# A graph network on one core: epsilon inside the square roots, a first phase begun by the features and not the lists, six chains there, and padding that isn't gathered

## The reference

```python
x = layernorm(x + attention(x, src, dst))         # Q, K, V = x W + b, 8 heads of 16
#   score = exp(clip(sum(K[src] * Q[dst]) / 4, -5, 5)); segment_sum(V[src] * score) / (segment_sum(score) + 1e-6)
x = layernorm(x + gin(x, src, dst, edge_attr_64)) # messages (x[src] + mlp(edge_attr)) / sqrt(deg deg), node mlp,
#   out * rsqrt(mean(out * out) + 1.19e-7) * rms_w
x = layernorm(x + equivariant(x, edge_attr_3, edge_weight, src, dst))
x = layernorm(x + gat(x, src, dst))               # exp(leaky(f_src[src] + f_dst[dst]) - segment_max), f_v[src]
layernorm(x) = (x - mean(x)) / sqrt(var(x) + 1e-5)
```

## Time and profile before

| | us |
|---|---|
| median of 3 runs (lowest, highest) | 4626.52 (4621.08, 4627.65) |
| the profiled execution | 4619.58 |
| its span, first to last instruction | 4614.9 |
| first gather to last gather, pass 1, 2, 3, 4 | 59.1 to 1098.5, 1181.3 to 2235.9, 2356.8 to 3396.9, 3469.7 to 4509.6 |
| first load of x (ACT's queue), issue | 0.71 |
| loads of x1, x2, x3 (SP's queue), issue | from 0.72, 4.83 in all |
| second and last load of the lists (SP's queue), issue | 12.93 |

### The profile page before, as it was taken

How to read it: one execution, slowest core, us unless ns; L and a number is a source line. 1 busy time by engine, 2 the same in 40 slices (tenths; PEclk the granted TensorE clock), 3 DMA queues, 4 the chain that set the end, 5 groups by cost and what they waited for, 6 DMA issues and landing times.

```text
span 4614.9 us, 103452 instructions
## 1 busy us (share of the span) xinstructions
PE 3700.7 (80%) x25659; PEld 3147.4 (68%) x25659; DVE 3313.9 (72%) x7588; ACT 2856.1 (62%) x7389; POOL 3271.2 (71%) x3435
## 2 busy tenths in 40 slices
PE   6888888887376666666769888888888999999996
PEld 4555555555376666666658677677677888888886
DVE  4666666667554444444668777777787999999998
ACT  3777676766532222222357666666656888888886
POOL 4777777775677777777657777777747777777772
PEclk8898898888587777777879999999999999999998
DMA  7888888884443333333122222222228887888882
GB/s 231 246 234 239 236 233 239 236 236 146 112 100 76 82 81 77 82 77 81 42 62 57 57 56 56 56 56 57 56 76 243 236 235 234 235 235 234 234 235 77
DMA packets 645495, 677.23 MB, mean 147 GB/s; under 512 B 126761, under 2 KB 511295, under 8 KB 645247
## 3 DMA queue, kind: packets, MB, share of 16 engines
q0 software_dynamic: 133120, 327.79, 27.2%
q1 hardware_dynamic: 509838, 346.88, 25.1%
q10 hardware_dynamic: 2416, 1.18, 0.1%
HBM read 584.73 MB, written 89.08 MB: 146 GB/s over the span
## 4 chain that ended last, share of the span: by engine, by line
POOL 27%; issue 21%; PE 16%; DVE 12%; ACT 11%; DMA 7%; SPq 2%; ACTq 2%; DVEq 1%; POOLq 0%
POOL e_rows L852 19%; POOL xt L852 8%; PE banks L914 7%; DVE acc L938 5%; ACT e_away L891 4%; DMA xt<-up_t,e_index 3%; PE banks L1032 3%; DVE banks L1482 2%; ACT e_logit L1478 1%; ACT banks L1544 1%; DMA e_q_rows<-q_t 1%; DMA e_rows<-kv_t,e_index 1%; ACTq L944 1%; ACT e_rows L1543 1%; PE banks L437 1%
## 5 line engine op out<-in xcount | busy, mean ns | idle before, releaser
L938 DVE TENSOR_TENSOR acc<-acc,banks 128x256 f32 x3328 | 1383.3, 416 | 886.1 <-PE banks L914 749.3
L852 POOL DMA_INDIRECT xt<-up_t,e_index x800 | 757.3, 947 | 243.7 <-issue 213.0
L852 POOL DMA_INDIRECT e_rows<-x_t,e_index x772 | 730.3, 946 | 248.0 <-issue 232.8
L852 POOL DMA_INDIRECT e_rows<-fsv_t,e_index x772 | 730.1, 946 | 236.0 <-issue 217.9
L852 POOL DMA_INDIRECT e_rows<-kv_t,e_index x772 | 730.1, 946 | 235.3 <-issue 220.7
L1174 ACT ACTIVATE e_rows<-banks,e_rows 128x128 f32<-128x128 f32 x832 | 236.9, 370 | 726.5 <-DMA e_rows<-x_t,e_index 481.0
L914 PE MATMUL banks<-e_sel,e_msg 128*128 128x128 f32 (+1 forms) x3328 | 654.5, 312 | 0.0
L1165 PE MATMUL banks<-e_w,xt 65*128 65x128 f32 x1664 | 273.2, 317 | 350.8 <-DMA xt<-in_attr_rows 346.7
L914 PEld LDWEIGHTS banks<-e_sel,e_msg 128*128 128x128 f32 (+1 forms) x3328 | 356.3, 148 | 262.6 <-issue 171.3
L891 ACT ACTIVATE e_away<-node_iota,local 128x128 f32<-128x128 f32 x1664 | 526.0, 388 | 0.0
L1165 PEld LDWEIGHTS banks<-e_w,xt 65*128 65x128 f32 x1664 | 248.6, 229 | 359.5 <-issue 308.0
(11 more groups left out here) (193 smaller groups left out, 7046.3 us busy)
## 6 DMA issues: line engine op xcount, KB each, us to landing
e_q_rows<-q_t SPq DMA_DIRECT2D x832, 64.0 KB
sel_d<-e_sel_t SPq DMA_DIRECT2D x208, 256.0 KB
e_sel_t<-sel_d SPq DMA_DIRECT2D x208, 256.0 KB
e_far<-fdst_t SPq DMA_DIRECT2D x832, 64.0 KB
e_near<-near_d SPq DMA_DIRECT2D x208, 128.0 KB
xt<-in_attr_rows SPq DMA_DIRECT2D x208, 128.0 KB, 3.6
e_resets<-reset_d SPq DMA_DIRECT2D x208, 128.0 KB
xt<-up_t,e_index POOLq DMA_INDIRECT x800
```

The lines of the kernel that those rows point to most:

```text
L852: G.indirect_dma_start(out=self.rows[:, u, i, 0:self.width], out_offset=None, in_=self.table, in_offset=bass.IndirectOffsetOnAxis(ap=index ...
L938: V.tensor_tensor(to, to, bank[n_bank][:, col:col + W].rearrange("p (k d) -> p k d", k=2), ALU.add).then_inc(self.s_added[i], 1)
```

## The change

Four edits. **Roots:** the scale is now ACT's immediate scale and the epsilon its bias column, made once by POOL (`ln_eps`, `rms_eps`); the instruction on DVE and its step in the plan are gone. **First phase:** the weights go first on ACT's queue, in three groups with a semaphore each (keys and values, their biases, the queries' own); all loads of x go on SP's queue, and the two loads of the integer rows (the lists) stand behind the first two of them. The planner gives the lists a start of 8.0 and the key/value chains 0.0, and there are six chains and not three. **Padding:** in the last group the chunk without edges isn't gathered, and of the chunk with 10 edges only 10 rows are. The wait for a group's rows counts the gathers that there are.

```diff
     def tables(...):
-        for lo, sem in zip(range(0, FULL_TILES, X_TILES), loaded_x):
-            (SP if lo else A).dma_start(x[:, lo:lo + X_TILES, :], ...).then_inc(sem, 16)
+        load_w(0, "k", loaded_kv)
+        load_w(1, "v", loaded_kv)
+        load_b(0, "k", loaded_b)
+        load_b(1, "v", loaded_b)
+        load_w(2, "q", loaded_q)
+        load_b(2, "q", loaded_q)
         G.memset(x[:, FULL_TILES:, :], 0.0).then_inc(cleared_x, 1)
-        SP.wait_ge(cleared_x, 1)
-        SP.dma_start(x[0:REST, FULL_TILES, :], ...).then_inc(loaded_x[-1], 16)
-        for n, name in enumerate(("k", "v", "q")):
-            A.dma_start(w_qkv[:, n * D:(n + 1) * D], ...).then_inc(loaded_qkv, 16)
-            A.dma_start(b_qkv[:, n * D:(n + 1) * D], ...).then_inc(loaded_qkv, 16)
+        load_x(SP, 0)
+        load_x(SP, 1)
         wait(SP, m_ints)
         d_ints.did(SP.dma_start(ints[:, 0:whole, :], ...))
         ints_in = d_ints.did(SP.dma_start(ints[0:rest, whole, :], ...))
+        load_x(SP, 2)
+        load_x(SP, 3)
+        SP.wait_ge(cleared_x, 1)
+        SP.dma_start(x[0:REST, FULL_TILES, :], ...).then_inc(loaded_x[-1], 16)
...
     def inverse_root(self, of, factor, eps, ready):
-            yield V, 0.15
-            wait(V, *ready)
-            m = self.v.did(V.tensor_scalar(col, of, factor, eps, ALU.mult, ALU.add))
             yield A, 0.25
             self.enter(A)
-            wait(A, m)
-            m = self.act.did(A.activation(root_of, col, ACT.Sqrt))
+            wait(A, *ready)
+            m = self.act.did(A.activation(root_of, of, ACT.Sqrt, bias=eps[:], scale=factor))
...
-            chain_free, engine_free = [0.0] * bool(also) + [begin] * n_streams, {e: 0.0 for e in ENGINES}
+            chain_free, engine_free = [also_begin] * bool(also) + [begin] * n_streams, {e: 0.0 for e in ENGINES}
...
-                    PE.wait_ge(loaded_qkv, 96)
+                    PE.wait_ge(loaded_kv, 32)
...
-        node_phase("proj0", make, 3, lambda ctx, closing: tables(...), 6.0, lambda ctx: own_made.append(...))
+        def queries(ctx):
+            for e in (PE, V):
+                e.wait_ge(loaded_q, 32)
+            own_made.append(project_own(ctx, w_qkv[:, 2 * D:], b_qkv[:, 2 * D:], q_t))
+
+        node_phase("proj0", make, 6, lambda ctx, closing: tables(...), late=queries, also_begin=8.0)
...
+    def edges_of(g, i):
+        return P if not isinstance(g.n, int) else min(P, max(0, N_EDGES - (g.n * GROUP + i) * P))
...
     def gather(self, g, s_free, s_ahead=None, lead=0):
+                n = edges_of(g, i)
+                if not n:
+                    continue
-                index = self.index[:, at:at + 1] if from_ring else src_c[:, ...]
-                G.indirect_dma_start(out=self.rows[:, u, i, 0:self.width], ...
+                index = self.index[0:n, at:at + 1] if from_ring else src_c[0:n, ...]
+                G.indirect_dma_start(out=self.rows[0:n, u, i, 0:self.width], ...
...
     def have_rows(self, engine, g):
-            engine.wait_ge(self.s_rows[...], (g.turn(self.slots) + 1) * 64)
+            engine.wait_ge(self.s_rows[...],
+                           g.turn(self.slots) * 64 + 16 * sum(edges_of(g, i) > 0 for i in range(GROUP)))
```

More of the change, by code:

```diff
@@ L205, in build @@
     node_iota = sb(root, "node_iota", [P, P])
-    ones_col = sb(root, "ones_col", [P, 1])
+    ones_col, ln_eps, rms_eps = (sb(root, n, [P, 1]) for n in ("ones_col", "ln_eps", "rms_eps"))
     minus_node = sb(root, "minus_node", [P, 1])
@@ L262, in tables @@
         m3 = g.did(G.memset(ident[:], 0.0))
-        g.did(G.memset(ones_col[:], 1.0))
+        for to, value in ((ones_col, 1.0), (ln_eps, LN_EPS), (rms_eps, RMS_EPS)):
+            g.did(G.memset(to[:], value))
         m_zeros = g.did(G.memset(zeros[:], 0.0))
@@ L293, in tables @@
             yield PE, 0.14 * (hi - lo)
[L294 to L295 removed]
+            PE.wait_ge(made_ident, 1)
             wait(PE, ready, *copied[n - 2:n - 1])
@@ L413, in layernorm @@
                 m = self.v.did(V.bn_aggr(self.mean_var[:, j, :], self.stats[:, j, :]))
-            m = yield from self.inverse_root(self.mean_var[:, 0:self.size, 1], 1.0, LN_EPS, [m])
+            m = yield from self.inverse_root(self.mean_var[:, 0:self.size, 1], 1.0, ln_eps, [m])
             wait(V, m)
@@ L446, in project2, with node_phase @@
             return done
-    def node_phase(tag, make, n_streams=STREAMS, also=None, begin=0.0, late=None):
+    def node_phase(tag, make, n_streams=STREAMS, also=None, begin=0.0, late=None, also_begin=0.0):
         with Phase(nc, tag, earlier) as ctx:
@@ L517, in project0 @@
         loaded_x = [nc.alloc_semaphore(f"loaded_x{n}") for n in range(FULL_TILES // X_TILES + 1)]
-        loaded_qkv, made_ident, cleared_x = (nc.alloc_semaphore(n) for n in ("loaded_qkv", "made_ident", "cleared_x"))
+        loaded_kv, loaded_b, loaded_q, made_ident, cleared_x = (
+            nc.alloc_semaphore(n) for n in ("loaded_kv", "loaded_b", "loaded_q", "made_ident", "cleared_x"))
         def make(k):
@@ L538, in make @@
             return steps
-        node_phase("proj0", make, 3, lambda ctx, closing: tables(ctx, closing, loaded_x, loaded_qkv, made_ident, cleared_x),
-                   6.0, lambda ctx: own_made.append(project_own(ctx, w_qkv[:, 2 * D:], b_qkv[:, 2 * D:], q_t)))
+        def queries(ctx):
+            for e in (PE, V):
+                e.wait_ge(loaded_q, 32)
+            own_made.append(project_own(ctx, w_qkv[:, 2 * D:], b_qkv[:, 2 * D:], q_t))
+        node_phase("proj0", make, 6, lambda ctx, closing: tables(ctx, closing, loaded_x, loaded_kv, loaded_b, loaded_q, made_ident, cleared_x),
+                   late=queries, also_begin=8.0)
     def after0():
@@ L662, in steps @@
                 m = k.v.did(V.tensor_reduce(k.small[:, 2, 0:k.size], sliced(sq, k), AX.X, ALU.add))
-                m = yield from k.inverse_root(k.small[:, 2, 0:k.size], 1.0 / D, RMS_EPS, [m])
+                m = yield from k.inverse_root(k.small[:, 2, 0:k.size], 1.0 / D, rms_eps, [m])
                 yield V, 1.2
@@ L850, in gather @@
                 at = (g.u % self.per_round) * GROUP + i
-                index = self.index[:, at:at + 1] if from_ring else src_c[:, g.n * GROUP + i:g.n * GROUP + i + 1]
-                G.indirect_dma_start(out=self.rows[:, u, i, 0:self.width], out_offset=None, in_=self.table,
+                n = edges_of(g, i)
+                if not n:
+                    continue
+                index = self.index[0:n, at:at + 1] if from_ring else src_c[0:n, g.n * GROUP + i:g.n * GROUP + i + 1]
+                G.indirect_dma_start(out=self.rows[0:n, u, i, 0:self.width], out_offset=None, in_=self.table,
                                      in_offset=bass.IndirectOffsetOnAxis(ap=index, axis=0)
```

20 lines of the change are left out of this document (12 added, 8 removed).

## The result

| | before | changed |
|---|---|---|
| median of 4 runs (us) | 4624.59 (4621.08 to 4627.65) | 4596.63 (4595.30 to 4599.02) |
| the profiled execution, its span | 4619.58, 4614.9 | 4596.9, 4592.8 |

The ratio is 0.9939, 95% interval 0.9927 to 0.9951: 28 us faster.

A forecast was written before the change was run, and what follows sets the result against it. It took POOL's gathers, 1.25 us each, to bound the edge passes, and DVE or cross-engine chains the node phases except the third (PE). -11.5 - 5.1 - 1.8 - 0.5 = -18.9 from 4626.5 gives 4608 us, range 4597 to 4620.

The forecast's parts named there:

- The roots' term: Node phases: removing DVE's 65 square-root instructions saves stalls and pitch, less ACT's added bias cost: -5.1 us.
- ceiling of 13.4: Node phases: most the removed DVE instructions could give, 9.2 us of stalls plus 52 x 0.08 of pitch.
- The first phase's term: Ahead of the first pass: PE starts earlier, first gather at 47.6 in place of 59.1: -11.5 us.
- rival a: First phase: x1 lands late, so the phase gives only 6 us; 4613 us in all, chance 0.12.
- the banks: First phase: one bank per chain makes matmul pairs wait for adds; six chains cover it, at worst 3 us of stalls.
- The cover: First pass: queries are needed only 35 us after the first gather, leaving 16 us, so the gain goes through whole.
- Rival (d): Edge passes: earlier gathers fall behind again by index reloads or queries, only roots and padding stay; 4619 us, chance 0.07.
- The worst case of this term: First phase: x1 landing at 13 us behind SP's stalled issue, with 3 us of single-bank stalls: -6 us.
- Rival (b): Node phases: POOL's lock stalls other DVE instructions with two SBUF operands, roots give 0.5; 4612 us, chance 0.13.
- the sign given for it: Last node phase: the 1.26 us pairs ahead of L410 gone, none longer than 0.2 on L416 and L756.
- Rival (c): Node phases: the reciprocal on DVE waits for unready roots, costing 32 us in place of gaining 5.1; 4645 us, chance 0.04.
- Padding, -1.8 and -0.5: Ends of passes: the last rows come earlier, -1.8 us in the second, -0.5 in the third, 0 in first and fourth.

The follow-up runs named there:

- g4: The kernel before with only the square roots' edit (epsilon as ACT's bias, DVE's instruction and the planner's step gone): 4612.66 us, ratio 0.9965.
- i1: The changed kernel with the planner's step for the root on ACT at 0.40 in place of 0.25: ratio 0.9934, on a slower chip.
- h4: The changed kernel with 60 one-column fills on DVE in its idle first 14 us: 4599.92 us, ratio 0.9940.
- f3: The kernel before with only the square roots' edit, but the planner keeping its 0.15 step on DVE: 4619.23 us, ratio 0.9987.

## Why the prediction was wrong, point by point

**The roots' term, -5.1, is the step that failed: it measured -16** (g4, 11 to 21; by the table's stages the node phases gain 19.2 and the fourth pass's drain takes 3.3 of it back). It was made of what DVE holds: stalls and pitch of 52 instructions, priced where DVE is the bound. Two sentences in it went wrong. "Of the 4.2 us of pitch, a third lies on a DVE that is the bound", where no row stood behind the third, and "The planner's weights lose 0.15 per root, so all four phases are interleaved anew; I give that no sign." The second node phase has 26 of the 65 roots, two in a row in each block's chain, and no full engine. There the hop from DVE to ACT and the place in DVE's queue count, not only DVE's own time: some 2 us by the instruction, 6.4 by the order, and 2 to 4 more by both together. With no sign and no size for the order, the ceiling of 13.4 was no ceiling. Why the new order is better in the second phase isn't worked out instruction by instruction; i1 shows only that it isn't the luck of one order.

**The first phase's term, -11.5, was right at its own place and wrong at the end.** First PE instruction, PE's stretch, tail and first gather came within 0.6 us each; x1 wasn't late (rival a), and the banks cost 0.2. "So the gain goes through whole" failed. The cover that was looked at (queries, 16 us) held; what took 5 to 6 of the 10.3 us back was the drain of the same pass, by a wait in DVE's code and PE's clock behind it. Rival (d) named falling behind again, by another cause. The worst case of this term, x1 at 13 us, leaned on SP's stalled issue; in the changed kernel SP issues the first two loads in 1.26 us, and PE starts at 10.35.

**Rival (b), locks moving on**, was half true in the last node phase: 3.2 of L396's 6.4 us came back on L428 and L774, and the sign given for it ("none longer than 0.2") was not met (1.24 and 1.67 us). That phase gained 4.3 us in the mean all the same. By the second half of the Trainium skill's rule that the prediction cites (SBUF — State Buffer, "Who interferes with whom"), instructions with two SBUF inputs are what waits, and these two are. In the second phase the same instruction got shorter: 7.28 us as L416, 4.51 as L428.

**Rival (c), slower,** didn't come: L415, the reciprocal, waited 13 times for 9.7 us, L403 11 times for 12.9. ACT's root went from 0.205 to 0.297 us, in the forecast's 0.28 to 0.30.

**Padding, -1.8 and -0.5:** the second pass's gathers and drain together are 5.9 us shorter, of which the 3.0 of the drain and the one gather of 1.25 go with the edit by the comparison above; the rest isn't settled. Third pass 0.4, within what two profiles of one kernel differ by.

**Errors of opposite signs.** By the table's means the kernel gained 27.2 us, 8.3 more than the sum: the roots' term was 11 too small, the first phase's 6 to 7 too large, padding with the rest of pass 2 some 4 too small. That the total is only 9 us off is in part this cancelling, so luck. The forecast's profiled time of 4600.7 is only 3.8 us off, since before's one profiled execution was faster than all its timed runs and the changed kernel's was not; and the 6.9 us that were carried over from the profile to the median don't exist in the changed kernel (4596.9 profiled, 4596.63 median).

## What to carry to other kernels

In a phase where no engine is full, price a removed instruction by its hop in the chain and by the order that the planner makes without it, and give the order a size by building the two halves apart: same order less the instruction, and new order with it. An earlier start is worth only what is left at the end of the stage behind it; look at the drain's pace and at waits marked "issue", on every engine, in unrolled code behind a hardware loop. Where a profile's waits move without a reason in the data, count the instructions ahead of them: a handful of fills is a cheap test.

## What the runs showed of the hardware that was not expected

- DVE stood for 3.1 to 4.3 us at one place behind the end of its first hardware loop in every kernel at the gathers' pace: near instruction 578 or 706 of its program, and in h4 near 690. Five one-column fills moved it by 34 us.
- After such a wait (PE idle for 3.5 us, 1.00 granted before) PE ran at a granted clock of 0.50 for some 8 us, and a group took 5.8 to 6.1 us in place of 3.8. ACT has waits of this kind too (2.72 us in f3's first pass, 2.56 in the changed kernel's fourth), with the same fall behind them (0.56, 0.66).
- On two of the five chips of the experiments this kernel took 25 and 27% longer, all of it in its edge passes and none in its node phases (second node phase 110.5 us there, 110.8 elsewhere).
